# Two stacked adaptive-norm blocks on one core: the feed-forward's norm statistics taken by ScalarE and GpSimd in place of VectorE, with a new merge table

## The reference, cut to what matters

```
x = x + ga * mixer0(norm(x) * (1 + ca) + sa)      # layer 0: a state-space scan, 512 channels x 16 states
x = x + gb * ffn0(norm(x) * (1 + cb) + sb)        # router softmax over 8, expert 7: gelu(h W1 + b1) W2, times its probability
x = x + ga * mixer1(...)                          # layer 1: a delta scan over 16 heads, then a norm
x = x + gb * ffn1(...)                            # norm, gated attention part, norm, bids of 3 experts, argmax, 2 wide experts

def norm(x):                                      # over the 256 channels of a token
    m = mean(x); v = var(x)
    return (x - m) / sqrt(v + 1e-5)

# mixer0's scan, one step for a channel d and a state s:
h = exp(dt * A[d, s]) * h + dt * B[s] * z ;  y += h * C[s]
```

## Time and profile before

| | |
|---|---|
| median of 3 executions | 3337.84 us |
| the profiled execution | 3338.62 us, of it the span of the trace 3336.8 us |
| PE busy | 2895.6 us (87%) |
| DVE busy | 2755.6 us (83%) |
| ACT busy | 2087.7 us (63%) |
| POOL busy | 1909.6 us (57%) |
| chain that ended last, by engine | PE 44%, DVE 22%, issue 14%, ACT 10%, POOL 6% |

### The profile page before, as it was taken

The page is one execution under the profiler, slowest core; times in us unless marked ns, Lnnn a source line. Parts: engine busy times, 40 slices in busy tenths (PEclk is TensorE's granted clock), DMA queues, the critical chain, the costliest instruction groups (busy, mean ns, idle before and its releaser), DMA issues.

```text
span 3336.8 us, 45399 instructions
## 1 busy us (share of the span) xinstructions
PE 2895.6 (87%) x14848; PEld 2382.9 (71%) x14848; DVE 2755.6 (83%) x4627; ACT 2087.7 (63%) x3843; POOL 1909.6 (57%) x1533
## 2 busy tenths in 40 slices
PE   5457689898999989899989989899998989898898
...
GB/s 239 42 39 84 32 92 105 70 118 46 124 85 113 94 93 112 79 95 63 117 99 111 92 79 117 61 122 67 118 92 102 105 81 112 47 108 124 42 133 44
DMA packets 152770, 308.57 MB, mean 92 GB/s; under 512 B 18364, under 2 KB 96980, under 8 KB 135124
## 3 DMA queue, kind: packets, MB, share of 16 engines
...
## 4 chain that ended last, share of the span: by engine, by line
PE 44%; DVE 22%; issue 14%; ACT 10%; POOL 6%; DVEq 0%; DMA 0%; POOLq 0%; ACTq 0%; SPq 0%
PE ps_B L1696 10%; PE ps_B L1801 8%; DVE hs L1475 8%; DVE acc L1439 8%; PE ps_A L1696 8%; PE ps_H L1691 7%; PE ps_H L1709 3%; POOL bu L1078 3%; PE ps_B L1691 3%; POOL z L1119 3%; PE ps_B L1845 2%; PE ps_B L1709 2%; ACT ps_A L1259 2%; DVE hA L1667 1%; ACT hid L1311 1%
## 5 line engine op out<-in xcount | busy, mean ns | idle before, releaser
L1078 POOL TENSOR_TENSOR bu<-z,bb 128x512 f32<-128x512 f32 x1024 | 1294.8, 1287 | 241.1 <-DVE hs L1475 134.7
L1475 DVE TENSOR_TENSOR_SCAN hs<-ps_A,state,bu 128x512 f32<-128x512 f32 x768 | 976.0, 1276 | 21.4 <-ACT ps_A L1259 13.5
L1259 ACT ACTIVATE ps_A<-dt,a_neg 128x512 f32<-128x512 f32 x1024 | 699.4, 686 | 419.3 <-DVE hs L1475 416.7
L1691 PE MATMUL ps_H<-ident,hs 128*128 128x128 f32 x4096 | 653.7, 294 | 220.5 <-DVE acc L1439 128.8
L1691 PEld LDWEIGHTS ps_H<-ident,hs 128*128 128x128 f32 x4096 | 528.4, 151 | 350.2 <-DVE acc L1439 156.3
L1439 DVE SCALAR_TENSOR_TENSOR acc<-ps_H,ctok,acc 128x512 f32<-128x512 f32 x960 | 702.0, 733 | 32.2 <-PE ps_H L1691 29.1
L1801 PE MATMUL ps_B<-ws_out,hid 128*128 128x256 f32 x2944 | 697.3, 381 | 10.6 <-ACT hid L1311 4.9
L1801 PEld LDWEIGHTS ps_B<-ws_out,hid 128*128 128x128 f32 x2944 | 538.2, 191 | 80.4 <-ACT hid L1403 9.4
L1696 PE MATMUL ps_B<-fh,ws_in 128*128 128x512 f32 x1440 | 542.1, 419 | 4.4 <-ACT rows_x L1276 4.0
L1475 DVE TENSOR_TENSOR_SCAN hs<-ps_A,bu 128x512 f32<-128x512 f32 x256 | 312.1, 1221 | 26.9 <-ACT ps_A L1259 20.7
L1696 PEld LDWEIGHTS ps_B<-fh,ws_in 128*128 128x128 f32 x1440 | 271.3, 188 | 60.0 <-ACT rows_x L1276 7.8
...
## 6 DMA issues: line engine op xcount, KB each, us to landing
ws_in<-w_split SPq DMA_DIRECT2D x126, 1024.0 KB, 4.9
bb<-b_rows SPq DMA_DIRECT2D x256, 256.0 KB, 3.7
...
w_split<-ws_in SPq DMA_DIRECT2D x8, 1024.0 KB, 5.0
...
```

What stands on the lines that cost most here:

```text
L1078: pool.tensor_tensor(bu[:, u % 4, :], z[:, d, :], bb[:, s % 2, :], ALU.mult)\
L1259: act.activation(b.t[:, :], dt[:, d, :], ACT.Exp, scale=a_neg[:, d, s:s + 1])\
L1475: dve.tensor_tensor_scan(hs[:, s % 2, d, :], b.t[:, :], bu[:, k % 4, :], state[:, s, d:d + 1] if i % CPB else 0.0, ALU.mult, ALU.add)\
L1691: return pe.transpose(dst, src, ident[:, :])
```

## The change

In `f_stream`, VectorE's piece `a_stats` is gone. ScalarE has two new pieces: `a_sum` copies x1 tile by tile into nF with the accumulator on, which gives the sum of each token; `a_sq` takes the square of x1 minus the mean, again with the accumulator. nF serves as scratch, and `a_norm` writes it afterwards as before. GpSimd has a new piece `mean_a` (minus the mean, from the sums), and `rstd_a` now also divides by 256 and adds eps. ScalarE now waits for x1 itself and twice for GpSimd. The kernel's first norm is taken in this way already (lines 1193 and 1198 with GpSimd's 1097 and 1100 to 1102).

```diff
                 def f_stream(j):        # GpSimd
+                    yield "mean_a"
+                    pool.wait_ge(f_sum.sem, f_sum.at(j, 1))
+                    pool.tensor_scalar(nm_f[:, :], sum_f[:, :], -1.0 / C, None, ALU.mult).then_inc(f_nm.sem, 1)
                     yield "rstd_a"
-                    pool.wait_ge(f_mv.sem, f_mv.at(j, 1))
-                    rstd_and_bias(rs_f, nm_f, nb_f, f_pow, f_pow.at(j, 1), f_rs)
+                    pool.wait_ge(f_sum.sem, f_sum.at(j, 2))
+                    pool.tensor_scalar(rs_f[:, :], sq_f[:, :], 1.0 / C, EPS, ALU.mult, ALU.add).then_inc(f_nm.sem, 1)
+                    pool.wait_ge(f_nm.sem, f_nm.at(j, 2))
+                    pool.tensor_tensor(rs_f[:, :], rs_f[:, :], mhalf[:, :], ALU.pow).then_inc(f_nm.sem, 1)
+                    pool.wait_ge(f_nm.sem, f_nm.at(j, 3))
+                    pool.tensor_tensor(nb_f[:, :], nm_f[:, :], rs_f[:, :], ALU.mult).then_inc(f_rs.sem, 1)
...
                 def f_stream(j):        # ScalarE
+                    yield "a_sum"
+                    since(act, f_x2, j)
+                    since_x1(act, j + 1)
+                    for t in range(NT):
+                        ins = act.activation(nF[:, t, :], xb[j % NX][:, t, :], ACT.Identity, accum_out=sum_f[:, t:t + 1])
+                    ins.then_inc(f_sum.sem, 1)
+                    yield "a_sq"
+                    act.wait_ge(f_nm.sem, f_nm.at(j, 1))
+                    for t in range(NT):
+                        ins = act.activation(nF[:, t, :], xb[j % NX][:, t, :], ACT.Square, bias=nm_f[:, t:t + 1],
+                                             accum_out=sq_f[:, t:t + 1])
+                    ins.then_inc(f_sum.sem, 1)
                     yield "a_norm"
-                    since(act, f_x2, j)
                     act.wait_ge(f_rs.sem, f_rs.at(j, 1))
...
                     x1 = xb[j % NX]     # VectorE
-                    yield "a_stats"
-                    since_x1(dve, j + 1)
-                    stats(own, x1, st_f, mv_f, rs_f, f_mv, nm_f)
```

All numbers of `PACE` are replaced; two of its lines:

```diff
-        21, "a_norm": 92, "h1T0": 96, "h1T1": 99, "h1h0": 100, "h1h1": 105, "router": 112, "lexp": 120, "c0":
+        "softplus3": 22, "a_sum": 92, "a_sq": 92, "a_norm": 94, "h1T0": 96, "h1T1": 96, "h1h0": 96, "h1h1": 97,
```

More of the change, by code:

```diff
@@ L164 @@
     "sp": {
[3 rows of a table removed]
-        282, "last_mod_x": -52, "last_rv": 177, "last_sw": 177, "last_e0_0": 177, "last_e0_1": 177,
-        "last_e0_0_down": 197, "last_e0_1_down": 202, "last_e1_0": 202, "last_e1_0_down": 220, "last_e1_1": 220,
-        "last_e1_1_down": 226, "last_out": 303,
[3 rows of a table added]
+        282, "last_mod_x": -65, "last_rv": 171, "last_sw": 171, "last_e0_0": 186, "last_e0_1": 304,
+        "last_e0_0_down": 309, "last_e0_1_down": 316, "last_e1_0": 320, "last_e1_0_down": 334, "last_e1_1": 345,
+        "last_e1_1_down": 350, "last_out": 350,
     },
     "pool": {
-        "mean0": -49, "rstd0": -35, "h0": -29, "mean1": -22, "rstd1": -12, "gx": 17, "u0": 22, "u1": 23, "u2":
-        23, "u3": 24, "xg": 39, "rstd_a": 109, "x_prob": 146, "rstd_e": 175, "h2": 200, "x_bias": 202, "rstd_h":
-        214, "rstd_i": 214, "rstd_j": 216, "rstd_m": 238, "x5": 282, "last_rstd_e": 151, "last_h2": 154,
-        "last_x_bias": 154, "last_rstd_h": 171, "last_rstd_i": 171, "last_rstd_j": 179, "last_rstd_m": 225,
-        "last_x5": 225,
+        "mean0": -44, "rstd0": -38, "h0": -30, "mean1": -16, "rstd1": -10, "gx": -1, "u0": 19, "u1": 22, "u2":
+        25, "u3": 27, "xg": 39, "mean_a": 98, "rstd_a": 105, "x_prob": 147, "rstd_e": 181, "h2": 192, "x_bias":
+        194, "rstd_h": 204, "rstd_i": 206, "rstd_j": 213, "rstd_m": 237, "x5": 282, "last_rstd_e": 158,
+        "last_h2": 169, "last_x_bias": 169, "last_rstd_h": 169, "last_rstd_i": 178, "last_rstd_j": 178,
+        "last_rstd_m": 290, "last_x5": 325,
     },
     "act": {
[17 rows of a table removed]
[17 rows of a table added]
     },
     "dve": {
[3 rows of a table removed]
-        203, "ao0": 207, "ao1": 208, "h_stats": 208, "h_norm": 208, "i_stats": 208, "i_norm": 208, "j_stats":
[4 rows of a table removed]
-        164, "last_ao0": 164, "last_ao1": 167, "last_h_stats": 179, "last_h_norm": 179, "last_i_stats": 179,
[4 rows of a table removed]
[3 rows of a table added]
+        "ao1": 196, "h_stats": 196, "h_norm": 196, "i_stats": 196, "i_norm": 196, "j_stats": 201, "lowx0": 213,
[4 rows of a table added]
+        "last_ao1": 180, "last_h_stats": 180, "last_h_norm": 180, "last_i_stats": 180, "last_i_norm": 180,
[4 rows of a table added]
     },
     "pe": {
[4 rows of a table removed]
[4 rows of a table added]
         184, "h2T1": 184, "kq0": 185, "kq1": 186, "kq2": 188, "kq3": 189, "kvT0": 191, "kvT1": 191, "btT0": 193,
[18 rows of a table removed]
[18 rows of a table added]
     },
@@ L384, in build @@
         nm_s, nb_s = sb("nm_s", [P, NT]), sb("nb_s", [P, NT])
-        st_f, mv_f, rs_f = sb("st_f", [P, NT, 6]), sb("mv_f", [P, NT, 2]), sb("rs_f", [P, NT])
+        sum_f, sq_f, rs_f = sb("sum_f", [P, NT]), sb("sq_f", [P, NT]), sb("rs_f", [P, NT])
         nm_f, nb_f = sb("nm_f", [P, NT]), sb("nb_f", [P, NT])
@@ L469, in build @@
         s_wog = signal("s_wog", 1)
-        f_mv = signal("f_mv", 1)
+        f_sum = signal("f_sum", 2)
         f_rs = signal("f_rs", 1)
         f_n = signal("f_n", 1)
-        f_pow = signal("f_pow", 1)
+        f_nm = signal("f_nm", 3)
         f_prob = signal("f_prob", 1)
@@ L1926, in _ @@
                 weave(PACE["pe"], step, n_stream, f_stream, x_stream)
-OWN = {"pool_n": 5, "dve_f": 8, "dve_x": 51}
+OWN = {"pool_n": 5, "dve_f": 3, "dve_x": 51}
 def kernel(**inputs):
```

## The result

The changed kernel takes 3320.2 us in the median of six executions against 3336.94 us before; the ratio is 0.9948 with a 95% interval of 0.9934 to 0.9961. One of the six ran slow throughout (3559.13 us at a mean granted clock of 0.81) and is left out of the ratio; the other five took 3316.43 to 3324.66 us, with a median of 3319.26. The kernel is 17 us faster. I had forecast 3340.0 us and no change to speak of: the time lies at the very edge of my range, and it moved the other way than my +1.4 us. The profiled execution has a span of 3319.3 us (before 3336.8).

What follows compares the result with a forecast made beforehand. TensorE, ScalarE and GpSimd were taken to bound the first three stages, VectorE and TensorE by turns the fourth. Terms 0 + 0 + 0.1 + 0 + 0.2 - 0.2 = +0.1 us a chunk, times 14 +1.4, gave 3340.0 us; range 3320 to 3360.

Steps and rivals of the forecast that it cites:

- The statistics at 0 on the path: First stage of a chunk: removing VectorE's 2.19 us a_stats saves 0, since TensorE does not wait for it.
- Rival A: VectorE paces everything, so 16 x 2.19 = 35 us go, giving 3304 us; chance 0.06.
- ScalarE's 3.57 us hidden: First stage: the added a_sum and a_sq fit where ScalarE idled 3.36 us, so bc's copy comes no later; 0.
- The front, +0.1: Stages before the scan's first read-out: delays from moved a_norm and h1T copies cost +0.1 us a chunk, within 0 and 0.6.
- `xn0`'s move: TensorE's order: transposes xn0 leave the place ahead of wo0 and stand before ao; 0, at best -0.2 us.
- the slack of 0.56 ahead of u8: Third stage: u8's scan waited 0.56 us for GpSimd; only delay beyond what VectorE's order can absorb reaches the scan.
- The loads, +0.2: SyncE's order: a row of B lands up to 2.45 us later behind a ws_out load; taken as +0.2 us a chunk.
- The end of the scan, -0.2: New places of small products where VectorE waits for TensorE save 0.2 us a chunk; ends -0.6 and 0.
- fourth stage: Rest of the scan and its close, 141.28 us a chunk; held untouched, a change over 1 us meaning the forecast is wrong.
- rival B: The scan's stage gets smoother: some 8 of 14 chunks spared the longer form, 12 us less, 3327 us; chance 0.22.
- C: ScalarE becomes the front's bound through moved a_norm and h1T copies: 1.4 us a chunk, 20 us slower, 3358; chance 0.25.
- D: The late row of B costs all of 1.7 us a chunk, 24 us slower, 3362; chance 0.07.

Runs made afterwards that it cites:

- e1: Changed kernel's new table of places with the old statistics, a_stats back on VectorE; 3316.31 us, ratio 0.9938 against the kernel before.
- e8: Changed kernel plus five unused VectorE statistics instructions per chunk, some 53 steps into the scan; 3335.41 us, ratio 1.0001 against the kernel before.
- e7: Kernel before, old table, with the new statistics and GpSimd's mean_a placed behind layer 1's h2 and x_bias; 3344.97 us, ratio 1.0033.
- e11: Changed kernel with SyncE's old numbers, so the old order of loads, except the last chunk's layer 1; 3321.2 us, ratio 0.9953.

## Why the prediction was wrong, step by step

- **The statistics at 0 on the path: right.** e1 puts VectorE's work back into the front, and the gain stays. Rival A, with the rule of the Trainium skill behind it ("Perfetto Trace Analysis", "Identifying the Most-Contended Engine"), is refuted for this edit: 35 us were not to be had. e8 shows that such work counts at one place of the scan.
- **ScalarE's 3.57 us hidden: right.** The two passes took 4.14 us with the hand-over, where 3.36 us of idle time and the 2.08 us of `a_norm` had been; `bc`'s copy still waited for TensorE.
- **The front, +0.1: right in size, by another way.** gate3's copy comes 0.17 us later behind the first sum (20.44 against 20.27), made of a `bc` that starts 0.29 earlier (6.04 against 6.33, where I gave `xn0`'s move 0 to 0.2) and a delay of 0.46 by `a_norm` (I said 0.35). softplus0 ends 0.18 later, where I said 0.4, and u8 0.12 later, where I said 0.1 (0.25 in the second trace). But the slack of 0.56 ahead of u8 was not the absorber that I took it for: it is 0.24 in the mean of the 14 chunks, and in e7 all of 0.41 went through. That made it no slack, but a wait for the very chain that was delayed.
- **The loads, +0.2: wrong, 0.** I reckoned with a slack of 0.78 us at one row of B. The waits for such rows doubled, and no difference that e11 can show came of it (3321.2 against 3319.13 us).
- **The end of the scan, -0.2, ends -0.6 and 0: too small.** It gave 0.61 and 0.40 in two traces, a part of it by the clock, for which the term had no reason.
- **The range.** The ends of the terms as I wrote them add up to -1.05 (-0.25 - 0.2 - 0.6) and +2.55 (0.25 + 0.6 + 1.7) us a chunk, not to -0.5 and +1.5. With -1.05 the low end is 3324 us, and the measured time lies below that, too.
- **The step that failed** is the sentence "I hold that it is untouched", of the fourth stage. I had named its 9 us of idle time as rival B's argument and held against it that "nothing in the change aims at the scan's own waits". But a table of which some 330 of 430 numbers differ (I had written all) needs no aim. u8 to u63 gave 0.40 + 0.51 us a chunk for which my sum had no term at all. 14 x 1.52 = 21 us of gain against 14 x 0.20 = 3 us of loss in front and closing make the result. My own sign of being wrong, more than 1 us in the fourth stage, shows in the means (1.44 us from u8 to the next first sum) but not in the one chunk (141.28 and 140.53). The order of TensorE's and ScalarE's pieces around u15 could have been read in both tables beforehand, with the 0.26 and 0.19 us of wait beside it in the trace.
- **Rival B: right in sign, right for a part of the gain.** I priced it at 12 us by sparing 8 of 14 chunks the long form. The long form is the longer stretch at half the clock, and it went from 10 chunks to 3 (5 in the second trace), so this part is real. The clock beside it, 0.97 and 0.98, was its mark, a small difference of the mean over a whole chunk. But the 0.91 us of gain from u8 to u63 are in long and short chunks alike, by the steps at u15, u43 and u57, and of the 1.17 us of `acc`'s wait ahead of kq, all gone, 0.51 came back at `sm`. That 12 us came near the 17 was partly luck.
- **Rivals C and D: no.** C's mechanism exists, as e7 measures (8 us), but not under the new table.

In the Trainium skill, "Perfetto Trace Analysis", section "Optimization Strategy", it says to look for the gaps of the engine in question within its regime and for what blocks it. For this kernel that rule points to where the gain lay: 29.1 us of VectorE's waits at `acc` were in the list of waits before the change, and 27 of VectorE's 32.2 us of idle time there are gone.
